# Eight-stage vision block on one core: one pair of experts to GpSimd, attention scores in packed tiles, half a normalisation to ScalarE

## The chip, the cores and the metric

The kernel runs on one core of one Trainium2 chip. The core has five engines that run side by side and meet at semaphores: TensorE (PE: matmuls, with its weight loads as PEld), VectorE (DVE), ScalarE (ACT), GpSimd (POOL) and SyncE (SP), which here issues all transfers. The metric is the device time of one execution in microseconds.

## The reference, cut

Eight residual stages run one after the other on a (4, 64, 128, 128) image: window attention, a choice feed-forward, a convolution with batch norm, a top-2 mixture of experts, four sweeps, a second choice feed-forward, sixteen dilated depthwise convolutions, a second top-2 mixture. The change touches the first, the fourth, the seventh and the eighth. All is float32.

```
# stage 1: 8x8 windows, 4 heads of 16 channels, shifted by 4
x = jnp.roll(x, (-SHIFT, -SHIFT), axis=(2, 3))
qkv = jnp.einsum('bchw,oc->bohw', x, qkv_w)
...
attn = jnp.einsum('wnqd,wnkd->wnqk', q, k) * SCALE
...
attn = attn + bias[None]
...
attn = jax.nn.softmax(attn, axis=-1)
out = jnp.einsum('wnqk,wnkd->wnqd', attn, v)
...
# stages 4 and 8: t = t + ffn(_ln_t(t)), 8 experts, 2 of them per token
router_probs = jax.nn.softmax(x @ router_w + router_b, axis=-1)
top_p, top_i = jax.lax.top_k(router_probs, K)
top_p = top_p / jnp.sum(top_p, axis=-1, keepdims=True)
expert_out = jnp.einsum('bnd,edc->bnec', x, expert_w) + expert_b
gathered = jnp.take_along_axis(expert_out, top_i[..., None], axis=2)
return jnp.einsum('bnk,bnkc->bnc', top_p, gathered)
...
# stage 7 starts with a norm over the 64 channels of each pixel
def _ln_c(v, eps=1e-06):
    m = jnp.mean(v, axis=1, keepdims=True)
    s = jnp.var(v, axis=1, keepdims=True)
    return (v - m) / jnp.sqrt(s + eps)
```

## The kernel before

Each stage is a function that writes one program per engine; between stages all engines meet at a barrier. The order on an engine is the order in which the code is written, and an engine waits in its place until the semaphore it needs has been counted up.

**Window attention** (`stage_window_attention`, 0 to 1404 us, tiles `wa_`). Two images share the 128 partitions (partition = 64 x image + channel). A strip is one row of 16 windows of both images; there are 2 x 16 strips, and each is four steps of four windows (`steps`). Step s on TensorE: `scores(s)` (L579), `qkv` of the next step (L567, L572), parts of the next strip's norm (`mean` L611, `variance` L620), `values` of step s-2 (L598), `turn_probs` of step s-1 (L588), `project` of step s-2 (L604), and at two places `turn_out` (L627). A window's scores are one matmul over all 128 partitions. So that it gives both images and four heads at once, ScalarE (`save_qk`) writes q twice, each time with the other image zeroed (`gmask`, L455), and k four times, each time with the other heads zeroed (`hmask`, L458). ScalarE then does `save_values` (L474), the softmax's exponential (L464), `save_probs` (L469), `save_proj` (L481), and pieces of the norm with two loads of its function table (L492, L498). VectorE adds the bias to the scores (L393), takes the maximum, subtracts it, sums and inverts (L404, L406). GpSimd multiplies by the inverted sums (L309), writes one copy of the normed input (L225) and adds the residual (L321, L322).

**Top-2 stages** (`stage_top2_ffn`, 2408 to 3166 us and 6490 to 7334 us, tiles `t_`). A beat handles 2048 tokens, there are 32 beats, and a beat has two halves i. Beat n on VectorE: `stats` of beat n+2 (L1668 to L1674), `route` of beat n+1 (L1695 to L1701), `norm` of n+2 (L1680, L1681), `gate` of n+1 (L1705 to L1710), then `weigh` of beat n: for each half the four pairs of experts q, each z(i, q) a product of 128 x 1024 (L1717) of the gates that a transfer has spread over the partitions (L1585) and the turned tokens `ht`. TensorE's `mix` (L1876) takes z(i, 0) to z(i, 3) in turn. ScalarE normalises beat n+2 (L1755), saves gates (L1773), turned tokens (L1763), logits and results (L1782, L1789), and does the square root (L1747) and the exponential (L1777), each behind a table load. In the second of the two stages GpSimd adds (`join`, L1645) the image of the stage before to the tokens; in the first it has no work.

**The norm of stage 7** (in `stage_spread`, 4996 to 5227 us). 64 steps, n = (tile of 8 columns, image). VectorE's order in a step: `total` of n+3 (L2589), `variance` of n+1 (L2597), `mean` of n+3 (L2593), and `scale` of n (L2602 and L2604), which writes 128 x 512 elements, spread in memory, into the resident image `y` (named `passes`). GpSimd centres n+3 once its mean is there (L2520); ScalarE takes the root (L2655) and the square (L2650). TensorE starts when all is scaled.

## Time and profile before

| | us |
|---|---|
| median of 3 runs | 7334.24 |
| lowest, highest | 7329.45, 7336.27 |
| the profiled execution | 7335.37 |
| span of its trace | 7333.6 |
| window attention | 1404 |
| first top-2 stage | 758 |
| norm of stage 7 | 231 |
| second top-2 stage | 844 |

The stages stand behind each other, so a gain in one is a gain in the total. The profile gives for each engine the time in which it was busy, for each group of instructions the count, the mean length and the idle time of the engine just before with the engine that ended it, and for any stretch a timeline. The profiled execution lies 1.1 us above the median.

### The profile page before, as it was taken

The page shows a single profiled execution, that of the slowest core. Times are in us where ns is not written, and L with a number is a line of the kernel's source. Part 1 is how long each engine was busy: PE and PEld are TensorE (multiplying, and loading weights), DVE is VectorE, ACT ScalarE, POOL GpSimd, SP SyncE. Part 2 cuts the span into 40 slices and gives each one's busy share as a digit, 9 for nine tenths or more (in the row PEclk, how much of TensorE's full clock was granted, in tenths as well). Part 3 has the DMA queues.
Part 4 walks back from the last instruction along what each step waited for, and adds up shares of the span by engine and source line. Part 5 has one row for each costly group of instructions (what it writes and reads, how often), then busy time and mean ns, then how long its engine had stood idle before and what let it go on. Part 6 is the DMA issues. An engine that isn't in the chain of part 4 may idle for free. (4 is left out here: it accounts for less than half of the span.)

```text
span 7333.6 us, 128704 instructions
## 1 busy us (share of the span) xinstructions
PE 5727.1 (78%) x43616; PEld 3801.7 (52%) x43616; DVE 4359.4 (59%) x8974; ACT 3789.7 (52%) x7044; POOL 1448.7 (20%) x1334
## 2 busy tenths in 40 slices
PE   6786777685499677759997999761499999957877
PEld 4565556425255333328997999241255555533333
DVE  5665656552822577783222344636877777768886
ACT  5665666551644566653224322421476777656664
POOL 2333333341512000041000000413211211121110
PEclk9888888885599788868998999865799999978888
DMA  0001000130323577740000022212566666637667
GB/s 25 27 27 30 18 24 27 42 88 4 95 83 86 181 239 229 239 132 29 0 0 0 0 80 92 80 37 78 90 86 82 74 84 87 83 88 216 211 217 212
DMA packets 793833, 645.41 MB, mean 88 GB/s; under 512 B 496193, under 2 KB 643841, under 8 KB 793421
## 3 DMA queue, kind: packets, MB, share of 16 engines
q1 hardware_dynamic: 792397, 639.01, 35.4%
q8 instruction: 241, 3.95, 0.2%
q14 instruction: 171, 1.40, 0.1%
q0 software_dynamic: 1024, 1.05, 0.1%
HBM read 549.73 MB, written 90.20 MB: 87 GB/s over the span
## 5 line engine op out<-in xcount | busy, mean ns | idle before, releaser
L2302 PE MATMUL sw_pC<-sw_row,sw_wc 128*128 128x128 f32 x10160 | 1158.1, 274 | 56.9 <-DVE sw_row L2177 54.9
L2302 PEld LDWEIGHTS sw_pC<-sw_row,sw_wc 128*128 128x128 f32 x10160 | 1147.6, 191 | 58.2 <-DVE sw_row L2177 55.5
L2723 PE MATMUL sp_pC<-sp_work,sp_bands 64*64 64x512 f32 (+11 forms) x14592 | 985.7, 428 | 43.5 <-issue 43.5
L2723 PEld LDWEIGHTS sp_pC<-sp_work,sp_bands 64*64 64x64 f32 x14592 | 598.2, 133 | 434.3 <-issue 366.1
L2165 DVE SCALAR_TENSOR_TENSOR sw_row<-sw_pC,sw_y 128x128 f32<-128x128 f32 x1016 | 337.0, 332 | 792.5 <-PE sw_pC L2302 792.5
L2663 ACT ACTIVATE sp_pC<-sp_pC,sp_par 128x512 f32<-128x512 f32 x832 | 597.7, 740 | 373.8 <-PE sp_pC L2723 348.0
L1717 DVE TENSOR_TENSOR t_z<-t_z,t_ht 128x1024 f32<-128x1024 f32 x512 | 630.6, 1297 | 18.6 <-DMA t_z<-gate_rows 18.1
L2234 ACT ACTIVATE sw_y<-sw_row 128x128 f32 (+1 forms) x762 | 265.2, 348 | 592.6 <-DVE sw_row L2165 592.6
L1876 PE MATMUL t_pO<-t_z,t_ew 128*64 128x512 f32 x2048 | 551.3, 685 | 4.0 <-DVE t_z L1717 3.1
L2626 DVE TENSOR_TENSOR sp_work<-sp_work,sp_pC 128x512 f32<-128x512 f32 x512 | 350.9, 687 | 169.7 <-ACT sp_pC L2663 169.2
L1846 PE MATMUL t_pT<-t_ident,t_h 128*128 128x128 f32 x1024 | 194.5, 352 | 263.6 <-ACT t_gs L1773 159.6
L309 POOL TENSOR_TENSOR wa_sc<-wa_sc,wa_sm 128x1024 f32<-128x1024 f32 x128 | 243.4, 1901 | 723.3 <-DVE wa_sm L406 723.3
L1005 PE MATMUL c_pG<-c_ht,c_gate_cols 128*32 128x512 f32 x512 | 290.4, 702 | 80.7 <-ACT c_ht L950 80.7
L579 PE MATMUL wa_pS<-wa_ks,wa_qs 128*128 128x256 f32 x1024 | 326.4, 475 | 22.0 <-issue 17.1
L1846 PEld LDWEIGHTS t_pT<-t_ident,t_h 128*128 128x128 f32 x1024 | 154.9, 181 | 325.2 <-issue 262.8
L1876 PEld LDWEIGHTS t_pO<-t_z,t_ew 128*64 128x64 f32 x2048 | 154.2, 159 | 322.4 <-issue 268.6
L1782 ACT ACTIVATE t_oc<-t_pO 128x512 f32<-128x512 f32 x128 | 76.6, 599 | 457.3 <-PE t_pO L1876 457.3
L579 PEld LDWEIGHTS wa_pS<-wa_ks,wa_qs 128*128 128x128 f32 x1024 | 248.5, 247 | 109.6 <-issue 62.9
L2534 POOL COPY sp_bands<-sp_bands 128x1536 f32<-128x1536 f32 x96 | 140.9, 1468 | 815.4 <-PE sp_pC L2723 778.1
L2663 ACT ACTIVATE sp_side<-sp_pC,sp_par 64x512 f32<-64x512 f32 x384 | 297.0, 773 | 7.5
L455 ACT ACTIVATE wa_qs<-wa_pQK,wa_gmask 128x256 f32<-128x256 f32 x256 | 107.3, 470 | 373.3 <-PE wa_pV L572 373.3
L393 DVE TENSOR_TENSOR wa_sc<-wa_pS,wa_bias 128x1024 f32<-128x1024 f32 (+1 forms) x128 | 147.8, 1155 | 248.9 <-PE wa_pS L579 245.8
(346 smaller groups left out, 10873.7 us busy)
## 6 DMA issues: line engine op xcount, KB each, us to landing
t_z<-gate_rows SPq DMA_DIRECT2D x512, 512.0 KB, 6.0
sp_bands<-windows SPq DMA_DIRECT2D x128, 512.0 KB
c_xs<-tokens SPq DMA_DIRECT2D x128, 256.0 KB, 2.6
cb_xs<-tokens SPq DMA_DIRECT2D x128, 256.0 KB, 2.8
wa_xs<-in_x SPq DMA_DIRECT2D x64, 256.0 KB, 2.8
tokens<-wa_xt SPq DMA_DIRECT2D x128, 128.0 KB, 2.1
tokens<-cb_h SPq DMA_DIRECT2D x64, 256.0 KB, 2.4
t_xs<-tokens SPq DMA_DIRECT2D x32, 512.0 KB, 9.2
```

The lines of the kernel that those rows point to most:

```text
L309: pool.tensor_tensor(p, p, r, ALU.mult).then_inc(probs_ready, 1)
L579: ins = pe.matmul(pS[:, w, :, :], qs[:, w, :, :].rearrange("p g q -> p (g q)"), ks[:, :, 64 * w:64 * w + 64], start=True, stop=True)
L1005: ins = pe.matmul(pG[m][E * b:E * b + E, :], gate_cols[:, m, :], ht[:, b % 2, :], start=True, stop=True)
L1717: dve.tensor_tensor(z[:, i, q, :], z[:, i, q, :], ht[:, m.k % HR, i, :], ALU.mult).then_inc(z_ready, 1)
L1846: ins = pe.transpose(pT[s][:, 128 * j:128 * j + 128], h[:, i, 4 * s + j, :, :].rearrange("p c d -> p (c d)"), ident[:, :])
L1876: ins = pe.matmul(pO[i][64 * s:64 * s + 64, :], ew[:, q, :], z[:, i, q, 512 * s:512 * s + 512], start=(q == 0), stop=(q == 3))
L2165: dve.scalar_tensor_tensor(row[par][c][:, :, PAD:PAD + P2], pC[c][:, 0:2 * P2].rearrange("p (b w) -> p b w", b=2), 0.0, line(sweep, c, i), ...
L2234: act.activation(line(sweep, c, i), row[par][c][:, :, PAD:PAD + P2], ACT.Copy).then_inc(saved[c], 1)
L2302: ins = pe.matmul(pC[c][:, 0:2 * P2], wc[:, sweep, m, :], row[1 - par][c][:, :, m:m + P2], start=(m == 0), stop=(m == 4))
L2626: return dve.tensor_tensor(new, old, rel, ALU.add)
L2663: return act.activation(out[rows_out, :], pC[q][rows_in, :], ACT.Relu, bias=par[rows_in, c, BI + i:BI + i + 1], scale=par[rows_in, c, SC + ...
L2723: ins = pe.matmul(out[halves[to], :, low * lo:low * hi], band[halves[k], (NV * g + j) % BANDS, q, AT[k][tap], :], v[halves[k], :, low * at ...
```

## The change

It has three parts.

**Window attention.** The scores of a window are no longer one matmul of 128 x 256, but four of 64 x 128: for each image g and each pair of heads hp one that reads only the 32 partitions of these channels and writes to 64 partitions of one half of `pS`. q is saved once, with a constant scale, and k twice (the two heads of a pair still need a mask). The four kinds of tiles count up `scores_ready` by four.

**Top-2 stages.** GpSimd multiplies z(i, 3), VectorE z(i, 0) to z(i, 2), and VectorE's products of the first half are placed between `stats`, `route`, `norm` and `gate`. GpSimd's `join` keeps its place ahead of the product of the same half, with the first three beats joined before the loop.

**Norm of stage 7.** VectorE scales the first four of a tile's eight columns, ScalarE the other four (four instructions of 128 x 64).

```diff
-        gmask = a.sb("gmask", [128, 2])
-        hmask = a.sb("hmask", [128, NH])
+        hmask = a.sb("hmask", [128, 2])
...
-        qs = a.sb("qs", [128, STEP, 2, 64])
-        ks = a.sb("ks", [128, NH, T])
+        qs = a.sb("qs", [128, T])
+        ks = a.sb("ks", [128, 2, T])
...
-        pS = a.ps("pS", [128, STEP, NH, 64])
+        pS = a.ps("pS", [128, 2, STEP, 128])
...
+                by_pair = e.rearrange("p w (a h) k -> p a w (h k)", a=2)
...
+                dve.tensor_tensor(by_pair[:, :, 0:n, :], pS[:, :, 0:n, :],
+                                  pairs[0].unsqueeze(2).to_broadcast([128, 2, n, 128]), ALU.add).then_inc(scores_read, 1)
...
-                for g in range(2):
-                    act.activation(qs[:, :, g, :], pQK[:, 0, :].rearrange("p (w q) -> p w q", q=64), ACT.Copy,
-                                   scale=gmask[:, g:g + 1])
-                for k in range(NH):
+                act.activation(qs[:, :], pQK[:, 0, :], ACT.Copy, scale=SCALE)
+                for k in range(2):
                     ins = act.activation(ks[:, k, :], pQK[:, 1, :], ACT.Copy, scale=hmask[:, k:k + 1])
...
                 for w in range(STEP):
-                    ins = pe.matmul(pS[:, w, :, :], qs[:, w, :, :].rearrange("p g q -> p (g q)"), ks[:, :, 64 * w:64 * w + 64],
-                                    start=True, stop=True)
-                ins.then_inc(scores_ready, 1)
+                    cols = slice(64 * w, 64 * w + 64)
+                    for g in range(2):
+                        for hp in range(2):
+                            o = 64 * g + 32 * hp
+                            ins = pe.matmul(pS[64 * g:64 * g + 64, hp, w, :], qs[o:o + 32, cols], ks[o:o + 32, :, cols],
+                                            start=True, stop=True)
+                            if w == STEP - 1:
+                                ins.then_inc(scores_ready, 1)
...
+            def join(m, i):
+                pool.wait_ge(x_in[0], 64 * m.n + 32 * i + 32)
+                pool.tensor_tensor(x_of(m, i), x_of(m, i), xs[:, :, :], ALU.add).then_inc(joined, 1)
+
+            def weigh_last(m, i):
+                pool.wait_ge(ht_saved, 4 * m.n + 2 * i + 2)
+                pool.wait_ge(g_in[i][3], 16 * m.n + 16)
+                pool.tensor_tensor(z[:, i, 3, :], z[:, i, 3, :], ht[:, m.k % HR, i, :], ALU.mult).then_inc(z_pool_ready, 1)
+
+            def beat(n):
+                for i in range(2):
+                    if rows is not None and n.plus(3).within(NB):
+                        join(n.plus(3), i)
+                    weigh_last(n, i)
...
-            def weigh(m, i):
+            def weigh(m, i, pairs):
                 dve.wait_ge(ht_saved, 4 * m.n + 2 * i + 2)
-                for q in range(4):
+                for q in pairs:
...
                     stats(n.plus(2))
+                weigh(n, 0, [0])
                 if route_due:
                     route(n.plus(1))
+                weigh(n, 0, [1])
                 if stats_due:
                     norm(n.plus(2))
+                weigh(n, 0, [2])
                 if route_due:
                     gate(n.plus(1))
-                for i in range(2):
-                    weigh(n, i)
+                weigh(n, 1, range(3))
...
-                    pe.wait_ge(z_ready, 8 * m.n + 4 * i + q + 1)
+                    if q < 3:
+                        pe.wait_ge(z_ready, 6 * m.n + 3 * i + q + 1)
+                    else:
+                        pe.wait_ge(z_pool_ready, 2 * m.n + i + 1)
...
-                dve.tensor_tensor(columns(n, b, t), h[:, b, :, :], bcast(s, TS), ALU.mult).then_inc(y_ready, 1)
+                dve.tensor_tensor(columns(n, b, t)[:, 0:TS // 2, :], h[:, b, 0:TS // 2, :], bcast(s[:, 0:TS // 2], TS // 2),
+                                  ALU.mult).then_inc(y_ready, 1)
...
+            def scale_rest(t, b, n):
+                act.wait_ge(inverted, n + 1)
+                for k in range(TS // 2, TS):
+                    ins = act.activation(columns(n, b, t)[:, k, :], h[:, b, k, :], ACT.Copy, scale=st[:, b, 1, k:k + 1])
+                ins.then_inc(rest_ready, 1)
+
+            pipelined(act, NT, [(root, 1), (square, 2), (scale_rest, 0)])
```

ScalarE, window attention, what `save_qk` issues in a step, first before and then after (`wa_pQK` holds q and k, `wa_qs` and `wa_ks` are the copies that TensorE reads):

```order
L455 ACTIVATE wa_qs<-wa_pQK,wa_gmask 128x4x64 x2
L458 ACTIVATE wa_ks<-wa_pQK,wa_hmask 128x256 x4
```

```order
L452 ACTIVATE wa_qs<-wa_pQK 128x256
L454 ACTIVATE wa_ks<-wa_pQK,wa_hmask 128x256 x2
```

Three of six instructions are gone.

VectorE, a beat of the first top-2 stage from the end of `route` on (`t_ex` is its last result, `t_sd` and `t_nm` are `norm`, `t_gt` to `t_gates` are `gate`), before:

```order
L1701 TENSOR_TENSOR t_ex<-t_mx 128x16
L1680 RECIPROCAL t_sd<-t_mom 128x16
L1681 SCALAR_TENSOR_TENSOR t_nm<-t_mom,t_sd 128x16
L1705 TENSOR_SCALAR t_gt<-t_ex 128x16
L1706 RECIPROCAL t_gt<-t_gt 128x16
L1707 TENSOR_TENSOR t_one<-t_one,t_ex 128x128
L1708 TENSOR_TENSOR t_one<-t_one 128x128
L1710 TENSOR_TENSOR t_gates<-t_one,t_gt 128x16x8
L1717 TENSOR_TENSOR t_z<-t_z,t_ht 128x1024 x8
```

and after, through the next `stats` to the start of the next `route` (the copy of `t_lg`):

```order
L1717 TENSOR_TENSOR t_ex<-t_mx 128x16
L1733 TENSOR_TENSOR t_z<-t_z,t_ht 128x1024
L1696 RECIPROCAL t_sd<-t_mom 128x16
L1697 SCALAR_TENSOR_TENSOR t_nm<-t_mom,t_sd 128x16
L1733 TENSOR_TENSOR t_z<-t_z,t_ht 128x1024
...
L1726 TENSOR_TENSOR t_gates<-t_one,t_gt 128x16x8
L1733 TENSOR_TENSOR t_z<-t_z,t_ht 128x1024 x3
...
L1690 TENSOR_TENSOR t_mom<-t_mom 128x16
L1733 TENSOR_TENSOR t_z<-t_z,t_ht 128x1024
L1711 COPY t_lg<-t_pX 128x64 x2
```

Of eight products behind the gates three are left; one stands ahead of `route`, one ahead of `norm`, one ahead of `gate`, and two have gone to GpSimd.

ScalarE, norm of stage 7, two steps (`sp_st` holds the means and variances, `sp_work` the centred tile and its squares), before and then after:

```order
L2655 ACTIVATE sp_st<-sp_st,sp_eps 128x8
L2650 ACTIVATE sp_work<-sp_work 128x512
L2655 ACTIVATE sp_st<-sp_st,sp_eps 128x8
L2650 ACTIVATE sp_work<-sp_work 128x512
```

```order
L2683 ACTIVATE sp_st<-sp_st,sp_eps 128x8
L2678 ACTIVATE sp_work<-sp_work 128x512
L2688 ACTIVATE passes<-sp_work,sp_st 128x64 x4
L2683 ACTIVATE sp_st<-sp_st,sp_eps 128x8
L2678 ACTIVATE sp_work<-sp_work 128x512
L2688 ACTIVATE passes<-sp_work,sp_st 128x64 x4
```

The four new instructions of a step stand ahead of the next step's root.

## Rows read from the trace of the kernel before

**Rows 1.** Windows, window attention: length, busy time (count) per engine, clock, DMA share, GB/s.
```profile
...
0.00:1404.00 1404.00, 1053.09 (x8444) 789.49 (x8444) 854.15 (x985) 843.82 (x1568) 463.74 (x301) 0.87 0.09 25
...
```

**Rows 2.** Timeline, window attention: start, length, engine, line, tiles, count, idle before.
```profile
...
501.27 1.90 POOL L309 TENSOR_TENSOR wa_sc<-wa_sc,wa_sm 128x1024 f32<-128x1024 f32 x1 [5.91 <-DVE wa_sm L406]
...
510.94 0.84 ACT L455 ACTIVATE wa_qs<-wa_pQK,wa_gmask 128x256 f32<-128x256 f32 x2 [2.58 <-PE wa_pV L572]
511.67 1.57 ACT L458 ACTIVATE wa_ks<-wa_pQK,wa_hmask 128x256 f32<-128x256 f32 x4
...
511.70 0.65 PE L598 MATMUL wa_pO<-wa_pt,wa_vs 128*32 128x64 f32 x32
...
513.10 0.42 ACT L474 ACTIVATE wa_ov<-wa_pO 128x256 f32<-128x256 f32 x1
...
518.40 1.97 PE L620 MATMUL wa_pL<-wa_sq,wa_mean_w 128*128 128x512 f32 x2 [4.13 <-ACT wa_sq L492]
...
```

**Rows 3.** Timeline, window attention, the steps that follow.
```profile
...
530.64 1.12 PE L627 MATMUL wa_pL<-wa_ident,wa_x 128*128 128x128 f32 x4 [2.61 <-POOL wa_x L322]
...
531.55 3.62 PE L579 MATMUL wa_pS<-wa_ks,wa_qs 128*128 128x256 f32 x8
...
539.83 0.70 PE L604 MATMUL wa_pO<-wa_ov,wa_w_cols 128*128 128x256 f32 x2 [0.61 <-ACT wa_ov L474]
...
540.37 1.89 PE L579 MATMUL wa_pS<-wa_ks,wa_qs 128*128 128x256 f32 x8
...
542.01 0.25 DVE L406 RECIPROCAL wa_sm<-wa_sm 128x16 f32<-128x16 f32 x1
...
```

**Rows 4.** Page part 5, convolution of the last stage: busy, mean ns, idle before.
```profile
...
L2723 PE MATMUL sp_pC<-sp_work,sp_bands 64*64 64x512 f32 (+11 forms) x14592 | 985.7, 428 | 43.5 <-issue 43.5
...
```

**Rows 5.** Timeline, first top-2 stage, one beat.
```profile
...
2725.55 0.25 DVE L1680 RECIPROCAL t_sd<-t_mom 128x16 f32<-128x16 f32 x1 [1.83 <-ACT t_mom L1747]
...
2727.56 0.17 DVE L1705 TENSOR_SCALAR t_gt<-t_ex 128x16 f32<-128x16 f32 x1 [1.55 <-ACT t_ex L1777]
...
2727.91 3.16 ACT L1755 ACTIVATE t_h<-t_xs,t_nm,t_sd 128x126 f32<-128x126 f32 x8
...
2728.75 9.15 DVE L1717 TENSOR_TENSOR t_z<-t_z,t_ht 128x1024 f32<-128x1024 f32 x8
...
2730.98 0.26 ACT L1773 ACTIVATE t_gs<-t_pT 128x128 f32<-128x128 f32 x1
...
```

**Rows 6.** Waits of the same stage, 2600 to 3000: us, times, longest.
```profile
...
PEld t_pO L1876 <- DVE t_z L1717: 6.7, 12, 0.6
...
```

**Rows 7.** Timeline, start of the same stage.
```profile
...
2458.39 0.22 DVE L1695 COPY t_lg<-t_pX 128x64 f32<-128x64 f32 x1 [9.26 <-PE t_pX L1861]
...
2463.22 3.18 ACT L1755 ACTIVATE t_h<-t_xs,t_nm,t_sd 128x126 f32<-128x126 f32 x8 [0.16 <-DVE t_nm L1681]
...
```

**Rows 8.** Line 1585 (gate transfers), from 2457: count, first and last start, landing.
```profile
...
L1585 SPq DMA_DIRECT2D t_z<-gate_rows x3: 530/606/607, 2458.4 to 2459.6; - x3
...
DMA to landing us min/median/max: 3.7/6.2/8.7
```

**Rows 9.** Timeline, second top-2 stage, a join beside products.
```profile
...
6897.90 6.05 DVE L1717 TENSOR_TENSOR t_z<-t_z,t_ht 128x1024 f32<-128x1024 f32 x4
6898.54 2.07 POOL L1645 TENSOR_TENSOR passes<-passes,t_xs 128x512 f32 x1 [4.89 <-DMA t_xs<-tokens]
...
```

**Rows 10.** Timeline, normalisation of the last convolution stage, two steps.
```profile
...
5105.69 1.04 POOL L2520 TENSOR_TENSOR sp_work<-sp_work,sp_st 128x512 f32<-128x512 f32 x1 [2.13 <-DVE sp_st L2593]
...
5105.85 1.75 DVE L2604 TENSOR_TENSOR passes<-sp_work,sp_st 128x512 f32 x1
...
5108.74 0.30 ACT L2655 ACTIVATE sp_st<-sp_st,sp_eps 128x8 f32<-128x8 f32 x1 [2.36 <-DVE sp_st L2597]
...
5109.03 1.75 DVE L2604 TENSOR_TENSOR passes<-sp_work,sp_st 128x512 f32 x1
```

**Rows 11.** Line 2604, all: form, count, shortest, median, longest ns.
```profile
...
L2604 DVE TENSOR_TENSOR passes<-sp_work,sp_st x64: 1016/1749/1864, 5029.5 to 5225.8; 128x512 f32 x56, 128x512 f32<-128x512 f32 x8
...
```

More of the change, by code:

```diff
@@ L290, in _ @@
             link = Link(pool, pool_done)
-            for s, k in ((x1_turned, 1), (yr_ready, 1), (qkv_ready, 1), (scores_ready, 1), (v_saved, 1), (pt_saved, 1),
+            for s, k in ((x1_turned, 1), (yr_ready, 1), (qkv_ready, 1), (scores_ready, 4), (v_saved, 1), (pt_saved, 1),
                          (proj_ready, 1), (scores_read, 1), (h_doubled, 1), (probs_turned, 2), (xt_saved, 2),
@@ L348, in _ @@
             dve.wait_ge(const_ready, 1)
-            for k, (bit, m) in enumerate([(5, 1), (2, 1), (4, 3), (6, 1)]):
+            for k, (bit, m) in enumerate([(5, 1), (2, 1), (4, 1), (6, 1)]):
                 link(dve.tensor_scalar(bits_q[:, k:k + 1], iota_q[:, :], bit, m, SHR, AND))
@@ L452, in save_qk @@
                 act.wait_ge(qkv_ready, s + 2)
-                act.wait_ge(scores_ready, s + 1)
-                for g in range(2):
-                    act.activation(qs[:, :, g, :], pQK[:, 0, :].rearrange("p (w q) -> p w q", q=64), ACT.Copy,
-                                   scale=gmask[:, g:g + 1])
-                for k in range(NH):
+                act.wait_ge(scores_ready, 4 * s + 4)
+                act.activation(qs[:, :], pQK[:, 0, :], ACT.Copy, scale=SCALE)
+                for k in range(2):
                     ins = act.activation(ks[:, k, :], pQK[:, 1, :], ACT.Copy, scale=hmask[:, k:k + 1])
@@ L1640, in _ @@
             pool.iota(order_i[:, :], pattern=[[-1, E]], base=E, channel_multiplier=0).then_inc(const_ready, 1)
+            def join(m, i):
[10 more added lines that the diff above has]
+                    weigh_last(n, i)
             if rows is not None:
-                def join(m):
+                for n in range(3):
                     for i in range(2):
-                        pool.wait_ge(x_in[0], 64 * m.n + 32 * i + 32)
-                        pool.tensor_tensor(x_of(m, i), x_of(m, i), xs[:, :, :], ALU.add).then_inc(joined, 1)
-                over_beats(pool, join)
+                        join(Beat(n, n, 0), i)
+            over_beats(pool, beat)
         @block.vector
@@ L1759, in save_turned @@
             def save_turned(m, i):
-                since(act, z_ready, 8 * m.n - 24 + 4 * i + 4)
+                since(act, z_ready, 6 * m.n - 18 + 3 * i + 3)
+                since(act, z_pool_ready, 2 * m.n - 6 + i + 1)
                 for s in range(2):
@@ L2513, in _ @@
             pool.sem_inc(y_ready, 4)
+            pool.sem_inc(rest_ready, 4)
             pool.sem_inc(var_ready, 2)
```

19 lines of the change are left out of this document (10 added, 9 removed).

## The prediction

> **What bounds the kernel now.** I read the busy time by stage first, because the three parts of the change lie in stages that follow each other: window attention is 1404 us of the 7333.6. No engine is full there: TensorE is busy 75% of the time, VectorE 61%, ScalarE 60% [rows 1]. So this stage is not bound by one engine's work, but by chains that pass from engine to engine, and what counts is whether an instruction lies on such a chain. The same holds for the top-2 stages, below. For that I read timelines and the idle time in front of single instructions.
>
> *Attention.* The 32 strips take 1404 / 32 = 43.9 us each, with filling and draining. In a strip I follow four steps. In the second (from 510.94) ScalarE never rests between `save_qk` and the norm's logarithm, and TensorE stands 4.13 us until that logarithm is there [rows 2]. Then ScalarE's root and GpSimd's two long operations lead to `turn_out`, before which TensorE waits 2.61 us, and behind it the scores of the fourth step run at the low clock, 3.62 us instead of 1.89 [rows 3]. Then `qkv`, `save_qk`, `save_values`, `project` (0.61 us idle before it) and the scores at 540.37 follow without a gap [rows 3]. VectorE closes a second loop: its inversion ends at 542.26, just as those scores end [rows 3].
>
> *Top-2.* VectorE rests in each beat 1.83 us for the root and 1.55 us for the exponential, both of ScalarE; the products follow at once [rows 5]. TensorE hardly waits for the products: 6.7 us in 400 [rows 6]. The loop that sets the beat runs over ScalarE and TensorE, and the gates need only be there when ScalarE saves them at 2730.98, behind a normalise that starts at 2727.91 [rows 5].
>
> *Norm of stage 7.* Here VectorE is the bound: one step is 5109.03 - 5105.85 = 3.18 us, and ScalarE rests 2.36 us of it [rows 10].
>
> **Attention, part by part.** *Scores.* Before: a step is 8 instructions (each float32 matmul makes two), 1.89 us at the high clock, 3.62 us at the low [rows 3]. After: 32 instructions of half the length (128 columns instead of 256). One after the other they would take 32 x 1.89 / 8 / 2 = 3.8 us. The four tiles of a window use different rows and columns of the array, and the pairs that share columns write to different halves of `pS`. Two rows bear on whether they run side by side. `values`: 32 instructions of 64 columns in 0.65 us [rows 2]; one by one they would need 32 x 1.89 / 8 / 4 = 1.9 us, so 2.9 run at once, the start included. The convolution's 64x64 tiles, which also share columns pairwise: 14592 instructions of up to 512 columns and 428 ns mean in 985.7 us, that is 6.3 under way at a time by their own lengths, four tiles with the next already queued [rows 4]. I take four at once, 3.8 / 4 = 0.95 us, a half of before. The bounds are 3.8 us (none at once) and 0.65 us (the shorter `values`).
>
> The Trainium skill ("TensorE: Matmul & The Clock Gate", measured speedup against the span model) gives 3.07 times, not 4, for four tiles of 32 rows. By it the scores would be 1.2 us and the sum below 0.6 us a strip smaller. No row here shows 32-row tiles.
>
> *ScalarE.* Three of six saves go. `save_qk` lasts from 510.94 to 513.24, 2.30 us [rows 2], so 1.15 us remain and 1.15 go. *VectorE* adds the same 1024 elements per partition in another order, at the same cost. *What of it is on the path*, step by step: fourth step, scores 3.62 / 2 = 1.8 us; `save_qk` 0.6 us, since TensorE stood only 0.61 before `project`, and then its own transposes are late next [rows 3]. First step: nothing, VectorE's inversion ends with the scores. Second step: scores 0.9 us; `save_qk` 0.7 us of 1.15, because `save_values` began at 513.10 and needs `values`, which end at 512.35 [rows 2]. Third step: nothing; the path goes through logarithm, root and GpSimd, beside scores and `save_qk`. The sum is 1.8 + 0.6 + 0.9 + 0.7 = 4.0 us a strip, 32 strips: **-128 us**. At most all 1.15 of three steps and 0.9 + 0.9 + 1.8 count, 7.0 us: -224. With two tiles at once only the 1.3 us of `save_qk` count: -42.
>
> **Top-2, part by part.** *Removed:* two products of VectorE per beat, 9.15 / 8 = 1.14 us each [rows 5]. VectorE is not late in the beat, so this brings 0. *Added on GpSimd:* two products of 128 x 1024, 1.90 us each as its other product of that size [rows 2], off the path as such. But GpSimd and VectorE hinder each other. In the second stage four VectorE products take 6.05 us beside one GpSimd addition of 2.07, where 4 x 1.14 = 4.6 are usual: one was held 1.4 us until GpSimd had ended [rows 9]. So GpSimd's 3.8 us a beat can cost VectorE up to as much, against 2.3 us taken off. The Trainium skill ("SBUF — State Buffer", SBUF: two separate sides) says it so: a GpSimd instruction and a VectorE one with two inputs in SBUF exclude each other for a whole instruction. The trace agrees, 1.4 us here.
>
> *Moved:* one product ahead of `norm` and one ahead of `gate`. They fill the 1.83 and 1.55 us in which VectorE stood [rows 5], which covers 1.14 each; if GpSimd holds one of them, up to 1.9 us more, `norm` comes at most some 1.2 us late. ScalarE takes its result only at 2727.91, 1.9 us after it was ready (2726.01), and the gates, ready at 2728.90, only at 2730.98 [rows 5]. So a steady beat costs **0**. If that cover goes, every us of delay is one per beat, 64 beats.
>
> *The start* costs. The first product now stands ahead of `route` of beat 1, which began at 2458.39 [rows 7]. Its gates were sent for at 2458.4 and landed at the earliest 3.7 us later [rows 8], at 2462.1. The product takes 1.14, the next another 1.14 ahead of `norm`, so normalise at 2463.22 [rows 7] moves by 3.7 + 1.1 + 1.1 = 6 us. Nothing gives that back. Two stages: **+12 us**.
>
> **Norm, part by part.** A step's scale takes VectorE 1.75 us, because it stands behind GpSimd's centring (5105.69 to 5106.73), and goes on 0.87 us after that [rows 10]. Without GpSimd beside it the same instruction takes 1.016 us [rows 11]. Half the elements save half of the 0.87: 0.43 us. ScalarE gets four instructions; 128 x 126 took 3.16 / 8 = 0.40 each [rows 5], so 1.6 us at most, into 2.36 us of idle less the 0.43: it fits by 0.3. GpSimd's centring of step n+4 now also waits for ScalarE's half of n, which ends some 2.5 us after the root has started, before the next mean. 61 full steps x 0.43 = **-26 us**. Bounds: 0 if ScalarE's four take 0.5 us each and it becomes the bound, -33 if all saved is 0.5 + some start.
>
> **Sum.** 7333.6 - 128 + 12 - 26 = 7191.6 for the trace's span; against the median 7334.2 - 142 = **7192**.
>
> **Rivals.**
>
> *Packing is only partial, or another wait is late next.* Attention gives 42 instead of 128: 7334 - 42 + 12 - 26 = **7278**. For it: 2.9 and not 4 at once in `values`, and more single instructions to issue. Against it: the convolution.
>
> *The tiles do not overlap: slower.* Place: TensorE's scores in every step. They would take 3.8 us at the high clock and 7.2 at the low: the fourth step loses 3.6, the first and second 1.9 each, less 1.3 from `save_qk`, 6.1 us a strip, 195 us: 7334 + 195 - 14 = **7515**. It decides from scores of about 1.25 times before (2.4 us); below that `save_qk` pays for it. The convolution's rows speak against it.
>
> *GpSimd's products delay the gates.* With two held operations and a product ahead of `gate`, it can pass the 2 us of cover by 1.5 us a beat: 64 x 1.5 = 96 us, **7288**. For it: the 1.4 us hold of rows 9. Against it: the products run when their transfers land, mostly beside instructions that have slack.
>
> *The clock stays low in attention.* TensorE ran there at 0.87 granted on average [rows 1], and after pauses at half. With shorter bursts it may fall in more places: `qkv`, `values` and transposes of two steps, some 4 us a strip, undo the gain: **7320**.
>
> **How the numbers follow.** Forecast 62%, partial packing 15%, delayed gates 13%, no overlap 5%, low clock 5%. The range reaches from stronger chains in attention (7 us a strip is the bound, 5 to 6 still likely: 7334 - 190 - 14, and some of the start's cost missing) to the delayed gates and the partial packing: 7115 to 7300. What counts as no change is 0.2%, 15 us, about what a measurement can tell. Of the cases only no overlap is slower, and the low clock lies near no change, on either side: faster 0.90, same 0.03, slower 0.07.
>
> **What would show it.** In the new trace: attention near 1276 us, 32 score instructions in 0.9 to 1.1 us at the high clock, ScalarE's saves 1.15 us; TensorE's wait before `project` gone and the wait of 4 us for the logarithm still there. Top-2 beats as long as before, VectorE idle more, the first normalise of beat 2 about 6 us late. Norm steps of 2.75 us. It is wrong if the scores last longer than 1.9 us, if the gates become what ScalarE waits for, or if the norm's step is set by ScalarE.

## The result and the profile after

| | before | after |
|---|---|---|
| median of 4 runs each, us | 7331.84 | 7219.48 |
| lowest, highest | 7328.12, 7336.27 | 7215.49, 7228.90 |
| the profiled execution's span | 7333.6 | 7213.8 |

The ratio is 0.9848, with a 95% interval of 0.9831 to 0.9865: 112 us faster. The forecast was 7192, a gain of 142, and the measured time lies inside its range. But the stages tell that this is partly luck. I read from both traces where the first instruction of each stage starts and list by how much each start moved:

| stretch | forecast | moved by |
|---|---|---|
| window attention | -128 | -113.4 |
| choice stage, convolution with batch norm | 0 | -3.3 |
| first top-2 stage | +6 | -7.9 |
| sweeps, second choice stage | 0 | +1.0 |
| stage 7 (its norm) | -26 | -26.3 |
| second top-2 stage | +6 | +30.1 |
| sum | -142 | -119.8 |

The norm is right to the microsecond, attention is 15 us short. The two top-2 stages go opposite ways, and neither does what I wrote.

Attention in the new trace. The view gives for stretches their length, busy time and count of PE, PEld, DVE, ACT and POOL, then the granted clock, the DMA share and GB/s (compare [rows 1]):

```profile
0.00:1294.00 1294.00, 965.63 (x11524) 697.29 (x11524) 847.09 (x981) 708.42 (x1186) 469.73 (x301) 0.86 0.10 27
```

ScalarE is relieved by 135 us and TensorE by 87, and the clock is as before, 0.86 against 0.87. The timeline of one strip (start, length, engine, line, instruction, count, idle before it and its releaser) answers to [rows 2, 3]:

```profile
467.24 1.10 PE L579 MATMUL wa_pS<-wa_ks,wa_qs 32*64 32x128 f32 x32
...
470.41 0.38 ACT L452 ACTIVATE wa_qs<-wa_pQK 128x256 f32<-128x256 f32 x1 [2.59 <-PE wa_pV L568]
470.69 0.83 ACT L454 ACTIVATE wa_ks<-wa_pQK,wa_hmask 128x256 f32<-128x256 f32 x2
...
477.08 2.04 PE L621 MATMUL wa_pL<-wa_sq,wa_mean_w 128*128 128x512 f32 x2 [3.88 <-ACT wa_sq L488]
479.05 1.99 PE L579 MATMUL wa_pS<-wa_ks,wa_qs 32*64 32x128 f32 x32
...
485.70 0.70 PE L605 MATMUL wa_pO<-wa_ov,wa_w_cols 128*128 128x256 f32 x2
...
489.39 0.66 PE L628 MATMUL wa_pL<-wa_ident,wa_x 128*128 128x128 f32 x4 [3.00 <-POOL wa_x L321]
489.98 1.85 PE L579 MATMUL wa_pS<-wa_ks,wa_qs 32*64 32x128 f32 x32
```

The scores take 1.10 us at a granted clock of 1.00 (467.24) and 1.99 and 1.85 at 0.50 and 0.55 (479.05, 489.98). The two saves end 1.1 us after the first starts (470.41 to 471.52). `project` (L605) has no wait any more. The waits for the logarithm (3.88) and for GpSimd (3.00) are still there. All of this was named beforehand.

Norm of stage 7, two steps, for [rows 10]:

```profile
4980.28 1.32 DVE L2630 TENSOR_TENSOR passes<-sp_work,sp_st 128x256 f32 x1
4980.71 1.10 ACT L2688 ACTIVATE passes<-sp_work,sp_st 128x64 f32 x4
...
4982.73 0.30 ACT L2683 ACTIVATE sp_st<-sp_st,sp_eps 128x8 f32<-128x8 f32 x1 [0.92 <-DVE sp_st L2623]
...
4983.02 1.32 DVE L2630 TENSOR_TENSOR passes<-sp_work,sp_st 128x256 f32 x1
```

A step is 4983.02 - 4980.28 = 2.74 us (forecast 2.75), and ScalarE still rests 0.92 us in it.

The first top-2 stage starts as forecast, only slower: VectorE stands for 13.12 us before its first product, `route` comes behind it, and the exponential waits for `route`.

```profile
2345.53 1.22 DVE L1733 TENSOR_TENSOR t_z<-t_z,t_ht 128x1024 f32<-128x1024 f32 x1 [13.12 <-DMA t_z<-gate_rows]
...
2350.82 0.21 ACT L1796 ACTIVATE t_ex<-t_ex 128x16 f32<-128x16 f32 x1 [5.89 <-DVE t_ex L1717]
2352.33 3.17 ACT L1773 ACTIVATE t_h<-t_xs,t_nm,t_sd 128x126 f32<-128x126 f32 x8 [1.30 <-DVE t_nm L1697]
```

And in the second top-2 stage the same happens again each time an image is finished, every eight beats, where the forecast had nothing (SPq is the queue in which SyncE issues transfers):

```profile
6810.77 14.52 SPq L1600 DMA_DIRECT2D out<-passes  x8
...
6825.33 1.53 SPq L1579 DMA_DIRECT2D gate_rows<-t_gs  x1
...
6830.06 2.50 SPq L1587 DMA_DIRECT2D t_z<-gate_rows  x4
...
6833.92 1.22 DVE L1733 TENSOR_TENSOR t_z<-t_z,t_ht 128x1024 f32<-128x1024 f32 x1 [10.73 <-DMA t_z<-gate_rows]
...
6839.22 0.21 ACT L1796 ACTIVATE t_ex<-t_ex 128x16 f32<-128x16 f32 x1 [6.26 <-DVE t_ex L1717]
...
6846.60 0.47 PE L1887 MATMUL t_pT<-t_ident,t_gates 128*128 128x128 f32 x1 [13.49 <-DVE t_gates L1726]
```

SyncE issues the eight transfers of `store` for 14.52 us. The gates of the next beat queue behind them, VectorE's product stands 10.73 us for them, `route` stands behind the product, and in the end TensorE stands 13.49 us for the gates.

### The profile page after: what moved, and what is told of

It reads as the page before. It is cut to its first block and busy times, and to the rows that moved or that the text cites. A ratio compares the mean times of both kernels' runs of the same rounds, so it can differ in the third digit from the quotient of the medians.

```text
span 7213.8 us, 135523 instructions
## 1 busy us (share of the span) xinstructions
PE 5637.2 (78%) x46688; PEld 3713.3 (51%) x46688; DVE 4357.5 (60%) x8842; ACT 3722.0 (52%) x6916; POOL 1826.4 (25%) x1462
## 5 line engine op out<-in xcount | busy, mean ns | idle before, releaser
L1733 DVE TENSOR_TENSOR t_z<-t_z,t_ht 128x1024 f32<-128x1024 f32 x384 | 590.0, 1563 | 173.3 <-DMA t_z<-gate_rows 162.8
L1651 POOL TENSOR_TENSOR t_z<-t_z,t_ht 128x1024 f32<-128x1024 f32 x128 | 373.5, 2918 | 630.3 <-DMA t_z<-gate_rows 630.3
L1646 POOL TENSOR_TENSOR passes<-passes,t_xs 128x512 f32 (+1 forms) x64 | 121.9, 1904 | 454.4 <-DMA t_xs<-tokens 454.4
```

What stands on the lines that cost most here:

```text
L1651: pool.tensor_tensor(z[:, i, 3, :], z[:, i, 3, :], ht[:, m.k % HR, i, :], ALU.mult).then_inc(z_pool_ready, 1)
L1733: dve.tensor_tensor(z[:, i, q, :], z[:, i, q, :], ht[:, m.k % HR, i, :], ALU.mult).then_inc(z_ready, 1)
```

## The experiments

The lengths below are in us, from one profiled execution each, from the end of the stage before to the end of this one by the arithmetic engines. So they differ by a few us from lengths between first instructions, and the second top-2 stage stands without the last 14 us, in which SyncE issues the final stores. The profiled execution isn't the median one: for the store behind the gates it is 19 us faster, for the stores one a beat 15 us, for the top-2 part alone 13 us slower.

Two executions of the same stage can differ: the choice stages, which no kernel touches, take 405 to 409 us in some traces and 413 to 416 in others, and the second top-2 stage with its code unchanged 821 to 829. Attention with its code unchanged takes 1398 to 1412, with the new code 1291 to 1298. So in these stages what is gained under 8 us, in attention under 14, is not to be read from this table. The first top-2 stage repeats better: 735, 735 and 736 in the three kernels that have the same code and the same place of the loop (below). The ratios are over all runs, each against runs of before that were made beside it, whose median lies between 7323.94 and 7331.84 us.

| kernel | ratio to before (95%) | attention | first top-2 | stage 7 | second top-2 |
|---|---|---|---|---|---|
| before | 1 | 1408 | 756 | 1498 | 823 |
| after | 0.9848 (0.9831 to 0.9865) | 1294 | 748 | 1472 | 853 |
| only attention | 0.9835 (0.9822 to 0.9848) | 1293 | 736 | 1500 | 828 |
| only norm | 0.9971 (0.9959 to 0.9983) | 1406 | 754 | 1473 | 824 |
| only top-2 | 1.0056 (1.0042 to 1.0069) | 1412 | 764 | 1501 | 855 |
| attention and norm | 0.9794 (0.9781 to 0.9806) | 1291 | 735 | 1473 | 821 |
| GpSimd's share, old order | 0.9818 (0.9805 to 0.9832) | 1297 | 737 | 1473 | 843 |
| new order, no share | 0.9823 (0.9808 to 0.9838) | 1293 | 742 | 1472 | 846 |
| after, store behind gates | 0.9857 (0.9840 to 0.9875) | 1293 | 746 | 1473 | 859 |
| after, stores one a beat | 0.9822 (0.9809 to 0.9835) | 1295 | 746 | 1473 | 833 |
| attention and norm, stores one a beat | 0.9794 (0.9781 to 0.9808) | 1298 | 735 | 1473 | 824 |
| attention and norm, saves back | 0.9895 (0.9880 to 0.9910) | 1351 | 754 | 1473 | 821 |
| attention and norm, filler | 0.9816 (0.9800 to 0.9833) | 1295 | 750 | 1472 | 829 |
| before, loop moved | 0.9973 (0.9963 to 0.9983) | 1398 | 739 | 1499 | 826 |

### The three parts, alone and in a pair

The edits are those of the change: its hunks in `stage_window_attention` alone, in `stage_top2_ffn` alone, in `stage_spread` alone, and the first and the last together.

> The kernel before with the attention part of the change alone. Theory (parts are additive, stages stand behind each other): the stage behind attention starts 113 us earlier, as it does in the trace of the changed kernel, so the whole kernel takes 7332 - 113 = 7219 us, ratio 0.985. My forecast for this part was -128 us. Rival (part of the gain of the changed kernel in attention comes from elsewhere, or attention changes what follows it): a value more than 10 us away from 7219.

> The kernel before with the top-2 part of the change alone. Theory: by the stage starts of the two traces the first top-2 stage gains 8 us and the second loses 30, so the whole takes 7332 + 22 = 7354 us, ratio 1.003. My forecast for this part was +12 us (7344). Rival (the loss in the second top-2 stage is an accident of that one trace, or comes from what runs ahead of it): no more than +12 us.

> The kernel before with the norm part of the change alone. Theory, and my forecast for this part: -26 us, 7306 us, ratio 0.9965, the norm's steps 2.75 us instead of 3.18. Rival (the convolution behind it starts earlier but waits for something else): nearer to 0.

> The attention part and the norm part together, the top-2 stages as before. Theory: -113 - 26 = -139 us, 7193 us, ratio 0.981, so 25 us or so faster than the whole change. Rival (the top-2 part is worth nothing or helps): 7219 or more.

Measured against 7323.94 us of before, in the order of the four texts: 7201.93 (-122), 7368.17 (+44), 7298.57 (-25), 7172.46 (-151). The norm is as expected. Attention gives 9 us more than the 113 that its own stage gave, and the top-2 part costs 44 and not 22. The table shows why: the attention part also shortens the first top-2 stage, from 756 (754 with the norm alone) to 736, a stage of which it changes no line. That gain had covered half of what the top-2 part costs. Without the attention part the first top-2 stage is 764 against 756, with it 748 against 735.

The pair without the top-2 part takes 7172.46 us, 0.9794, and is faster than before and than after.

### Where the first top-2 stage gained: the place of a loop

In the trace of before, ScalarE stands three times in this stage with nothing to wait for ("issue"), once at each jump back of its loop over six beats. This view lists what ended its idle time ahead of the normalise (us, times), from 2280 to 3200 us, first before, then attention and norm:

```profile
its engine sat idle before it (us, times) until:
  issue: 17.5, 3
```

```profile
its engine sat idle before it (us, times) until:
  DVE t_nm L1682: 0.8, 3
```

Attention's part takes three instructions out of each of the 32 written copies of `save_qk`, 96 in all. By a count in the built programs, ScalarE's loop of the first top-2 stage then stands at instructions 712 to 989 and not at 784 to 1061. That is 72 and not 96 earlier; what the other 24 are was not followed, but they are there with the saves back too (808 = 784 + 24, below). The count is not the chip's own: a turn of the loop has 277 instructions by it and leaves 313 records of ScalarE in the trace. Two kernels move the loop alone.

```diff
 # filler (attention and norm), ScalarE, ahead of the first top-2 stage
+            if rows is None:
+                for k in range(72):
+                    act.activation(y[:, 0, 0, k // 32, k % 32:k % 32 + 1], eps[:, 0:1], ACT.Copy)
             first = Beat(0, 0, 0)
             root(first)
```

> Attention and norm parts (without the top-2 part), with 72 one-column copies put on ScalarE ahead of the first top-2 stage, which do nothing for the result. They put ScalarE's loop of that stage back to where it stood in the kernel before, instructions 784 to 1061 of its program instead of 712 to 989. Theory (three pauses of about 6 us at the loop's jumps back depend on the place of the loop in ScalarE's program, and the attention part moved it by 72 instructions): three intervals of ScalarE's exponential in that stage grow from 20 to 26 us and the stage takes 735 + 17 + the copies' own time (0 to 15 us, they stand where ScalarE waits). Rival (the pauses have another cause in attention): no interval grows.

Measured: 7194.49 us, 0.9816 against 0.9794 of the same kernel without the copies. The stage grows from 735 to 750, and the pauses are back, three with 13.4 us together. The rest of the 22 us can lie in the second top-2 stage, where the pauses at the same jumps grow from 6.3 to 16.4 us (the stage from 821 to 829). Two of the three in the first stage:

```profile
2527.34 3.17 ACT L1756 ACTIVATE t_h<-t_xs,t_nm,t_sd 128x126 f32<-128x126 f32 x8 [4.96 <-issue]
...
2661.40 3.17 ACT L1756 ACTIVATE t_h<-t_xs,t_nm,t_sd 128x126 f32<-128x126 f32 x8 [3.90 <-issue]
```

The copies themselves lie in time in which ScalarE waits: 6.83 us, with 7.75 idle behind them:

```profile
2296.84 6.83 ACT L1827 ACTIVATE t_y<-t_eps 128x1 f32<-128x1 f32 x72 [19.84 <-POOL t_order_i L1641]
2311.42 0.31 ACT L1748 ACTIVATE t_mom<-t_mom,t_eps 128x16 f32<-128x16 f32 x1 [7.75 <-DVE t_mom L1675]
```

The last run asks the other way round: the kernel before, with nothing of the change, and its loop moved to a place that is like the good one.

```diff
 # before, loop moved: ScalarE, ahead of the first top-2 stage
+                for k in range(184):
+                    act.activation(y[:, 0, 0, k // 32, k % 32:k % 32 + 1], eps[:, 0:1], ACT.Copy)
```

> The kernel before, with 184 one-column copies put on ScalarE ahead of its work in the first top-2 stage. They do nothing for the result and take 184 x 0.095 = 17 us, of which some 15 lie in time in which ScalarE waits. ScalarE's loop of that stage then stands at instructions 968 to 1245 of its program, instead of 784 to 1061. The Trainium skill (Runtime: NRT & Kernel Launch, Instruction fetch mechanics) says that instructions are fetched in blocks of 256 and that a jump back out of the window stalls; 968 is 256 behind the 712 at which the loop stands with the attention part, so by blocks it stands as there. Theory (the place within the blocks decides): the three intervals of 26 to 27 us between ScalarE's exponentials shrink to 20 to 22, the stage takes 756 - 17 + 3 = 742 us and the whole 0.2% less than before, without anything of the change. Rival one (the pauses come from something in the attention part other than the place, or from the distance into the program): the three long intervals stay, ratio 1.000 or a little over.

Measured: 7309.37 us against 7329.56 of before beside it, 0.9973 (0.9963 to 0.9983), the stage 739 us (expected 742), and no pause. The 184 copies take 17.28 us, nearly all of it in time in which ScalarE waited: the first exponential comes 2 us later after the stage's start. It is the clearest result of the study: adding 184 instructions makes the kernel 20 us faster. The profile's list of DMA queues (packets, MB, share of the engines' time) shows the same from another side, for the stretch 2500 to 2960 us, first before, then the moved one, then the filler:

```profile
q14 instruction: 38, 0.31, 0.2%
```

```profile
q14 instruction: 23, 0.19, 0.1%
```

```profile
q14 instruction: 37, 0.30, 0.2%
```

Some 15 packets of instructions more where the pauses are, about five a jump. A packet is 0.31 MB / 38 = 8 KB. That q14 is ScalarE's queue is an inference from this agreement; the profile doesn't name the engine. The Trainium skill ("Runtime: NRT & Kernel Launch", Instruction fetch mechanics) says that the sequencer fetches ahead in blocks, and that a jump to a block outside its window stalls until it is fetched. The packets and the pauses agree. What these runs don't give is the rule for which places are good: the loop paused at 784, at 808 (saves back, below) and did not at 712 and 968, and in all four it is longer, with 277 instructions, than the 256 that this section of the Trainium skill gives for one block.

### The top-2 part: order or share

The part does two things to VectorE: two products go to GpSimd (share), and the products of the first half move between the small operations (order). Both kernels keep attention and norm.

```diff
 # share, old order: VectorE's beat
-                weigh(n, 0, [0])
...
-                weigh(n, 0, [1])
...
-                weigh(n, 0, [2])
                 if route_due:
                     gate(n.plus(1))
+                weigh(n, 0, range(3))
                 weigh(n, 1, range(3))
```

> The changed kernel, but VectorE's six products of a beat all stand behind gate again, as before the change; GpSimd keeps its pair. Theory (the top-2 loss comes from the product that stands ahead of route and waits there for its transfer, at the start and behind the three image ends): the loss is gone, the second top-2 stage takes about 821 us instead of 853 and the whole about as much as attention and norm together, ratio to the kernel before 0.979 to 0.981. Rival (the loss comes from GpSimd and VectorE holding each other, 2.9 us a GpSimd product and 1.6 to 1.8 us a VectorE one): the loss stays, ratio 0.984 to 0.985.

```diff
 # new order, no share: VectorE's beat, GpSimd as before the change
                 weigh(n, 0, [2])
                 if route_due:
                     gate(n.plus(1))
-                weigh(n, 1, range(3))
+                weigh(n, 0, [3])
+                weigh(n, 1, range(4))
```

> Attention and norm parts, and of the top-2 part the order alone: VectorE does all eight products of a beat, one each ahead of route, norm and gate. GpSimd multiplies nothing. Theory (the order causes the loss): ratio 0.984 to 0.985, the first top-2 stage +9 us and the second +30 against their lengths with the old order (735 and 821 us); in the second, waits of about 10 us for t_z behind each image end. Rival (mutual holding causes it): ratio 0.979 to 0.981.

Measured: 7196.54 us (0.9818) and 7201.58 us (0.9823). Against 0.9794 the share alone costs 0.24% or 18 us, the order alone 0.29% or 21 us, and both together (0.9848) 40. The two theories were put as rivals, and both are at work. By stages: the order costs 7 us in the first stage and 25 in the second, the share 1 and 22, both together 12 and 32.

The 22 and 25 us of the second stage don't add up to 32, and with the 8 us by which this stage differs from trace to trace neither is exact.

The order shows what the theory said, products that stand up to 13.2 us for their gates (waits of 6450 to 7150 us: us in all, times, longest):

```profile
PE t_pT L1872 <- DVE t_gates L1711: 73.0, 28, 11.4
...
DVE t_z L1718 <- DMA t_z<-gate_rows: 54.6, 20, 13.2
```

For the share the trace of the second stage, where GpSimd has `join` too, shows two mechanisms. How the 22 us divide between them was not measured. One: while GpSimd works, VectorE's small operations are held.

```profile
7065.29 1.74 POOL L1646 TENSOR_TENSOR passes<-passes,t_xs 128x512 f32<-128x512 f32 x1 [11.27 <-DMA t_xs<-tokens]
7065.61 1.56 DVE L1705 TENSOR_TENSOR t_one<-t_eq,t_mx 128x128 f32<-128x128 f32 x1
...
7066.98 2.42 POOL L1651 TENSOR_TENSOR t_z<-t_z,t_ht 128x1024 f32<-128x1024 f32 x1
7067.21 2.23 DVE L1717 TENSOR_TENSOR t_ex<-t_mx 128x16 f32<-128x16 f32 x1
```

The first ends at 7067.17 instead of 7065.90, and the second, 16 elements a partition, with GpSimd's product at 7069.4. Both are steps of `route`, on the way to the exponential. Such holds alone are not enough for a loss: in the first stage 10 executions of the first of these two instructions began beside GpSimd and all 10 were held, and the share costs 1 us there. Two: GpSimd's product stands behind `join` in its program (before the change nothing stood behind it), and `join` stands for tokens whose transfer queues behind `store`, which SyncE issued from 6992.38 for 14.60 us:

```profile
7023.97 1.64 POOL L1646 TENSOR_TENSOR passes<-passes,t_xs 128x512 f32 x1 [23.14 <-DMA t_xs<-tokens]
...
7025.56 3.33 POOL L1651 TENSOR_TENSOR t_z<-t_z,t_ht 128x1024 f32<-128x1024 f32 x1
...
7028.94 1.97 PE L1896 MATMUL t_pO<-t_z,t_ew 128*64 128x512 f32 x4 [3.27 <-POOL t_z L1651]
```

### SyncE's queue behind an image end

```diff
 # after, store behind gates: SyncE's loop
-                if n > 0:
+                if rows is None and n > 0:
                     store(n - 1)
...
                 if n + 1 < NB:
                     spread_gates(n + 1, 1)
+                if rows is not None and n > 0:
+                    store(n - 1)
```

> The changed kernel with one move on SyncE in the last stage: the eight transfers that store a finished image are issued behind the gate transfers of that beat instead of ahead of them. Theory (the gates' write and spread queue behind some 14 us of issuing, and VectorE's route stands behind the product that needs them): the three delays of 7 to 9 us behind the image ends vanish, the second top-2 stage takes some 853 - 25 = 828 us, ratio 0.9815; the start's 8 us in each stage stay. Rival (the delays come from the bandwidth that the stores take, not from the queue): the stage stays above 845 us.

Measured: 7222.12 us, 0.9857, and 859 us for the stage where 828 were expected. The theory had the queue right and the place wrong. (The profiled execution is the fastest of four, 7203.45 us.) The gates of this beat are out in time, but the next beat's tokens and gates now stand behind the store. `stats` and TensorE's `mix` wait for GpSimd, which waits for the tokens:

```profile
6610.75 17.96 SPq L1600 DMA_DIRECT2D out<-passes  x8
...
6628.76 3.82 SPq L1574 DMA_DIRECT2D t_xs<-tokens  x2
...
6637.03 2.79 DVE L1686 BATCH_NORM_STATS2 t_bs<-passes 128x6 f32 x16 [15.45 <-POOL passes L1648]
...
6639.24 1.97 PE L1900 MATMUL t_pO<-t_z,t_ew 128*64 128x512 f32 x4 [5.88 <-POOL t_z L1653]
```

So the block itself has to be broken up.

```diff
 # stores one a beat: SyncE's loop, behind the gates of the beat
+                if rows is not None and n >= W // J:
+                    store_piece(n // (W // J) - 1, n % (W // J))
```

> The changed kernel, but in the last stage the eight transfers that store a finished image are issued one a beat in the eight beats that follow, each behind the gate transfers, instead of all eight in one beat. Theory (what delays the beats behind an image end is that SyncE issues transfers for some 14 us in a row, wherever in the beat that stands, while gates and tokens queue behind): the three delays of 5 to 9 us go, the second top-2 stage takes 828 to 835 us instead of 853, ratio 0.981 to 0.982. Rival (the delays come from the memory traffic of the stores, or from the exclusion of the two engines alone): 850 us or more.

> Attention and norm parts with the top-2 stages as before, and the stores one a beat. Theory (with the old order the queue's 14 us are almost wholly hidden by slack; only the 1 to 2 us behind each image end remain): 3 to 6 us faster than attention and norm alone, ratio about 0.979. Rival (nothing was left there): the same ratio as attention and norm alone, 0.9794. Rival two (stores beside other beats take bandwidth from the gates' transfers): slower, 0.981 or more.

Measured: with the change 7195.36 us, 0.9822 instead of 0.9848, and the stage 833 us: the three delays are gone, the longest wait of a product in the steady stretch is 5.4 us and no longer 13.3. Without the top-2 part nothing comes of it, 0.9794 both times, where 3 to 6 us were expected. These two kernels also price the top-2 part without the block of stores: 0.9822 against 0.9794, 20 us, by the table 11 in the first stage and 9 in the second. In the second stage the intervals between ScalarE's exponentials differ by 6.3 us in all over the first two, the start, and by at most 0.8 us in any one after that. The holds are still there:

```profile
L1726 DVE TENSOR_SCALAR t_gt<-t_ex x64: 159/168/2098, 2321.2 to 7126.4; 128x16 f32<-128x16 f32 x64
```

Of these 64 executions 21 took over 0.3 us, as many as with the stores in one block, yet they lengthen no beat. So the steady beats of the second stage cover what GpSimd holds, as those of the first do, and the losses at the image ends, of the order and of the share alike, hang on the block. (The share with the old order and one store a beat was not run.)

In the kernel before, the same 14 us of issuing were covered: VectorE's products came last in its beat, and nothing that others wait for stood behind them.

### Attention: scores or saves

```diff
 # saves back: save_qk, with a tile that nobody reads
+                act.activation(idle[:, 0, :], pQK[:, 0, :], ACT.Copy, scale=SCALE)
                 act.activation(qs[:, :], pQK[:, 0, :], ACT.Copy, scale=SCALE)
+                for k in range(2):
+                    act.activation(idle[:, 1 + k, :], pQK[:, 1, :], ACT.Copy, scale=hmask[:, k:k + 1])
```

> Attention and norm parts, but ScalarE makes its three removed saves again, into a tile that nothing reads, ahead of the saves that are read; the scores stay packed. Forecast's theory (saves are worth 0.6 us in the fourth and 0.7 us in the second step of a strip, the rest of the gain is the scores'): attention takes 1291 + 32 x 1.3 = 1333 us. Rival (the saves' 1.15 us lie on the path in three steps): 1291 + 32 x 3.4 = 1401 us, so that the packed scores alone bring nothing. And by ScalarE's loop of the first top-2 stage, which now stands at instructions 808 to 1085 of its program: the three pauses of some 5 us are back, as in the kernel before.

Measured: 7248.11 us, 0.9895, attention 1351 us, between the two theories (1333 and 1401). The saves are worth 60 us, the scores 1408 - 1351 = 57, each to within some 7 to 14 us. From the starts of the scores in the three traces, the means of the four steps over 30 of the 32 strips (all but the last of each image):

| us | before | saves back | attention and norm | whole difference | forecast of it |
|---|---|---|---|---|---|
| first step | 8.55 | 8.13 | 7.82 | -0.7 | 0 |
| second | 12.74 | 12.14 | 11.72 | -1.0 | -1.6 |
| third | 11.02 | 11.14 | 10.80 | -0.2 | 0 |
| fourth | 9.13 | 8.26 | 7.42 | -1.7 | -2.4 |
| strip | 41.44 | 39.67 | 37.77 | -3.7 | -4.0 |

Two of TensorE's waits from 300 to 1000 us (in all, times, longest), before, with the saves back, and attention and norm:

```profile
PE wa_pL L627 <- POOL wa_x L322: 35.5, 16, 3.2
PE wa_pO L604 <- ACT wa_ov L474: 35.3, 61, 1.1
```

```profile
PE wa_pL L632 <- POOL wa_x L322: 43.1, 17, 3.2
PE wa_pO L609 <- ACT wa_ov L474: 25.4, 35, 1.0
```

```profile
PE wa_pL L628 <- POOL wa_x L321: 51.8, 17, 3.2
...
PE wa_pO L605 <- ACT wa_ov L470: 0.5, 1, 0.5
```

`project` waits for ScalarE's `save_values` as long as the three saves stand ahead of it, and hardly at all without them. At the same time TensorE waits longer for GpSimd's residual ahead of `turn_out`: part of what is gained elsewhere comes back there.

In the fourth step the shorter scores bring 0.87 us although they last up to 1.6 us less (3.62 to 1.98), and the saves 0.84. What covers the rest of the scores' gain in this step was not shown. The pauses of the top-2 loop are back as well (16.3 us, three times), the second place at which that was seen.

## Why the prediction was right or wrong, point by point

- **Scores, 0.95 us for 1.89.** Nearly. They take 1.10, so 3.8 / 1.10 = 3.4 tiles run at once, where I took four. By the 3.07 times of the Trainium skill ("TensorE: Matmul & The Clock Gate", Measured speedup vs the span model) the estimate was 1.2 us. The trace lies between the two. The rival "packing is only partial" fell, and "the tiles do not overlap" with it.
- **Saves, 1.15 us less.** Right: 1.1 us remain.
- **What of it is on the path.** The sum of 4.0 us a strip was 3.5 in the changed kernel (37.90 instead of 41.44), 3.7 in the one above, and with 3.5 the stage gained 113 us instead of 128. The terms that failed are the second and the fourth step: 1.6 forecast and 1.0 found, 2.4 forecast and 1.7 found. The first and the third, forecast at nothing, gave 0.7 and 0.2. The split was wrong too. I gave 2.7 of the 4.0 us to the scores and 1.3 to the saves; the runs give 1.8 and 1.9. The worst single term is the scores of the fourth step, 1.8 forecast and 0.9 found. The mistake was to price each row by itself, in a loop where other waits grow when one shrinks.
- **A steady beat of the top-2 stages costs 0.** Right in the first stage, where GpSimd has no `join`: the share alone costs 1 us. In the second it is right for most beats and wrong for those behind the three image ends. The step that failed is "GpSimd's products, off the path as such": there they stand behind `join`, and its transfers behind `store`. With the block of stores in place the share costs some 22 us there. The rival of held gates had one part of it (a held small operation, a late `route`) but priced it at 1.5 us in every beat, 96 us. The holds came, and with one store a beat they cost no steady beat anything.
- **The product ahead of `route`.** I saw that it makes `route` wait for a transfer, and counted that once a stage, as a start. What I left out is that in the second stage the queue that brings this transfer is blocked for 14.5 us at three more places. The row for it was there in the profile (`store`, L1598 of before). The forecast followed SyncE's transfers only in the first stage, where `store` is one transfer a beat.
- **Start +6 each.** Measured 8.5 to 9 us in the first stage, by the intervals between ScalarE's exponentials in the first four beats, and 6 to 8 in the second, by which kernel one compares with. The rest is `route` itself, which now also comes behind the transfer, and the exponential waits for it (5.89 us).
- **GpSimd's product, 1.90 us.** Too little: 2.34 at the shortest, 2.9 in the mean. The row I took it from multiplies by a small tile, one value for many elements.
- **The clock.** 0.86 in attention against 0.87 before. That rival fell.
- **Norm, -26 us.** Right in every term, 2.75 us a step, -26.3 by the traces and -25 by the runs. It is the one place where a single engine was the bound: VectorE has no idle time in these steps, before or after.
- **Nothing else moves.** Wrong: 15 to 20 us of the gain come from the place of a loop in ScalarE's program, in a stage that the attention part doesn't touch. No row of before says that a move of the loop would end its pauses. But the three idle times marked "issue", 17.5 us ahead of the loop's first instruction, were there to be asked about.

Taken together, the traces lie 22 us above the forecast: +15 from attention, -14 from the first top-2 stage (some -20 from the loop's place, +6 because the part costs 12 there and not 6), +24 from the second, and -3 from the rest. Errors of both signs hid each other, and that the total came within 28 us of the forecast is partly luck.

## What to carry to other kernels

Ahead of an instruction that others wait for, put none that waits for a transfer, unless you have followed that transfer's queue through every phase of the kernel, the rare ones too. Here the eight transfers that came every eight beats in one block were such a phase; issued one a beat they cost nothing that the runs could tell (0.9794 both times). And before a gain or a loss is put down to an edit, look at stages that the edit doesn't touch: a loop may have moved in an engine's program. Adding instructions that do nothing, in a place where the engine waits, tells this apart.

## What the runs showed of the hardware

**Which of VectorE's instructions GpSimd holds.** In the kernel with GpSimd's share and the old order (count; ns shortest, median, longest):

```profile
L1704 DVE TENSOR_REDUCE t_mx<-t_eq x128: 285/286/288, 2329.2 to 7135.6; 128x16 f32<-128x128 f32 x128
```

```profile
L1705 DVE TENSOR_TENSOR t_one<-t_eq,t_mx x128: 291/291/2424, 2329.6 to 7135.9; 128x128 f32<-128x128 f32 x128
```

```profile
L1696 DVE RECIPROCAL t_sd<-t_mom x64: 238/252/254, 2313.5 to 7114.9; 128x16 f32<-128x16 f32 x64
```

```profile
L1721 DVE TENSOR_SCALAR t_gt<-t_ex x64: 166/175/1974, 2332.3 to 7139.9; 128x16 f32<-128x16 f32 x64
```

```profile
L1651 POOL TENSOR_TENSOR t_z<-t_z,t_ht x128: 2340/2419/3439, 2356.4 to 7161.3; 128x1024 f32<-128x1024 f32 x128
```

Reductions and reciprocals were never held, though 18 of the reciprocals of the second stage ran beside GpSimd; of the reductions in `route` only 7 began beside it. Instructions with two inputs in SBUF were: of the second of these lines 15 began beside GpSimd and all 15 were held, up to 2.1 us for one of 0.29. So were 10 of 14 of the TENSOR_SCALAR, which has one tensor as input. GpSimd is held as well: 3.44 us instead of 2.34. The Trainium skill ("SBUF — State Buffer", SBUF: two separate sides) lists two inputs in SBUF and the two-port modes as what takes the shared ports. The rows agree for the two inputs. Whether this TENSOR_SCALAR ran in such a mode no row shows. The price for a tiny instruction is the lesson: its size doesn't protect it. One of 0.17 us took 2.23, until GpSimd's product had ended.

**A loop's place can cost 4 to 6 us a jump.** Shown above, with 0.27% of the whole kernel as its price. In the second top-2 stage, whose loop is longer (377 instructions against 277 by the same count), ScalarE pauses in every kernel at its three jumps, 6 to 11 us together, and 16 in the one with the filler. That was not explored.
